# A fixed place in a 20-place period for each background piece of the first attention of a gated two-layer kernel

## What is computed

```python
x = x + jnp.tanh(g_xattn[0]) * _L0_xattn_ref(_layernorm(x, axis=-1), ctx_1024, ...)
x = x + jnp.tanh(g_ffn[0]) * _L0_ffn_ref(_layernorm(x, axis=-1), ...)
x = x + jnp.tanh(g_xattn[1]) * _L1_xattn_ref(_layernorm(x, axis=-1), ctx_1024, ctx_1024)
x = x + jnp.tanh(g_ffn[1]) * _L1_ffn_ref(_layernorm(x, axis=-1), ...)
```

```python
q = query @ Wq.T + bq          # k, v from key_value in the same way
scores = jnp.einsum('bhqd,bhkd->bhqk', q, k) / np.sqrt(HD).astype(np.float32)
s = jnp.where(x >= 0, x + 1.0, 1.0 / (1.0 - x))
attn = s / jnp.sum(s, axis=-1, keepdims=True)
context = jnp.einsum('bhqk,bhkd->bhqd', attn, v)
return context @ Wo.T + bo
```

## Time and profile before

| | us |
|---|---|
| median of 3 runs | 1206.94 (1204.21 to 1207.81) |
| the profiled execution, device time | 1198.75 |
| its span, first to last instruction | 1196.9 |
| PE, DVE, ACT, POOL busy | 1012.3, 791.6, 624.9, 382.4 |
| first attention (28.4 to 339.8 us of the span) | 311.4 |
| its tail to the barrier (339.8 to 398.4 us) | 58.6 |

### The profile page before, as it was taken

One profiled execution on the slowest core, in us unless ns is written; L12 is line 12 of the kernel. 1 busy time (PEld: TensorE's weight loads), 2 busy tenths in 40 slices (PEclk: granted clock), 3 DMA queues, 4 the chain that ended last, 5 costly groups with the idle time before them and its releaser, 6 DMA issues.

```text
span 1196.9 us, 16849 instructions
## 1 busy us (share of the span) xinstructions
PE 1012.3 (85%) x5379; PEld 713.5 (60%) x5379; DVE 791.6 (66%) x2003; ACT 624.9 (52%) x1205; POOL 382.4 (32%) x385
## 2 busy tenths in 40 slices
PE   4898798698875679989899976888898988898988
PEld 2454454354444567878687754546575766666666
DVE  5777877866777757664657566776667577664443
ACT  2776656757846425564654431364555455544542
POOL 6000000000000013777767722224344343524134
PEclk9898979979997889999999995989999999999999
DMA  6654542632121433888877653331312232120001
GB/s 155 172 149 125 163 137 62 178 117 53 50 106 53 145 108 94 185 216 223 215 192 178 140 135 78 102 100 27 107 49 81 56 91 80 53 58 1 21 1 36
DMA packets 101559, 128.38 MB, mean 107 GB/s; under 512 B 31136, under 2 KB 73504, under 8 KB 101216
## 3 DMA queue, kind: packets, MB, share of 16 engines
q1 hardware_dynamic: 87088, 106.32, 31.1%
q0 software_dynamic: 12288, 18.88, 8.8%
q10 hardware_dynamic: 2096, 2.10, 0.8%
HBM read 66.15 MB, written 30.70 MB: 81 GB/s over the span
## 4 chain that ended last, share of the span: by engine, by line
PE 52%; DVE 27%; ACT 7%; issue 6%; POOL 3%; DMA 2%; ACTq 1%; SPq 1%; DVEq 0%; POOLq 0%
PE psum L951 5%; PE psum L1135 5%; PE psum L1120 5%; PE psum L1040 4%; PE psum L858 4%; PE psum L967 4%; PE psum L829 3%; DVE stats L1405 3%; DVE peaks L1815 3%; DVE weights L1530 3%; PE psum L904 3%; PE psum L818 2%; PE psum L1067 2%; PE psum L853 2%; PE psum L775 2%
## 5 line engine op out<-in xcount | busy, mean ns | idle before, releaser
L1914 POOL TENSOR_SCALAR vareps<-moments 128x4 f32<-128x4 f32 x32 | 10.4, 326 | 477.5 <-DVE moments L1414 477.5
L829 PE MATMUL psum<-q_stack,k_stack 97*128 97x512 f32 (+1 forms) x256 | 119.0, 493 | 38.6 <-DVE weights L1530 21.4
L1341 ACT ACTIVATE weights<-psum 128x512 f32<-128x512 f32 x160 | 92.9, 595 | 65.8 <-PE psum L829 57.5
L1934 POOL DMA_INDIRECT expert_sums<-made,sum_rows x64 | 103.3, 1614 | 61.1 <-DVE made L1779 42.6
L1067 PE MATMUL psum<-k_stack,q_stack 96*128 96x308 f32 x256 | 86.1, 397 | 36.4 <-DVE peaks L1815 24.2
L1530 DVE SCALAR_TENSOR_TENSOR weights<-weights,psum 128x512 f32<-128x512 f32 x160 | 101.8, 679 | 21.4 <-ACT weights L1196 21.3
L1815 DVE TENSOR_REDUCE peaks<-psum 128x2 f32<-128x308 f32 x256 | 105.6, 469 | 9.3 <-PE psum L1067 9.2
L1191 ACT ACTIVATE weights<-psum 128x512 f32<-128x512 f32 x160 | 88.8, 595 | 29.2 <-PE psum L829 28.9
L951 PE MATMUL psum<-feat_parts,w_shared_up 128*128 128x512 f32 x384 | 98.3, 406 | 6.4 <-DVE shared_silu L1653 2.8
L1966 POOL TENSOR_TENSOR hidden<-hidden_whole,hidden 128x512 fp32r<-128x512 f32 x64 | 82.9, 1300 | 61.0 <-DVE hidden L1863 61.0
L1135 PE MATMUL psum<-w_con_high,hidden 128*128 128x256 f32 x512 | 101.2, 296 | 0.5 <-POOL hidden L1966 0.5
(11 more groups left out here) (211 smaller groups left out, 2204.7 us busy)
## 6 DMA issues: line engine op xcount, KB each, us to landing
expert_w<-in_expert_w SPq DMA_DIRECT2D x64, 384.0 KB
q_stack<-q_stage SPq DMA_DIRECT2D x96, 128.0 KB, 2.4
q_stack<-q_stage SPq DMA_DIRECT2D x174, 64.0 KB, 2.0
expert_sums<-zeros SPq DMA_DIRECT2D x6, 1408.0 KB, 8.3
fetched<-expert_sums SPq DMA_DIRECT2D x14, 512.0 KB, 4.6
k_raw<-in_k SPq DMA_DIRECT2D x16, 300.0 KB
x<-in_x SPq DMA_DIRECT2D x8, 512.0 KB, 4.7
rows_scratch<-rows SPq DMA_DIRECT2D x8, 512.0 KB, 2.9
```

The lines of the kernel that those rows point to most:

```text
L829: T.matmul(to, keys_of(h, head), q[0:row, head // 2, :], start=True, stop=True).then_inc(scored, 1)
L1341: A.activation(weights1[n % 6][:, :], score_bank[n % 2], ACT.Exp).then_inc(exped, 1)
L1934: G.indirect_dma_start(sum_dram[e % SUMS], bass.IndirectOffsetOnAxis(ap=sum_rows[:, e:e + 1], axis=0), made[e % 4][:, :], None, bounds_che ...
```

## The change

The three streams are gone from the attention loop. Each step of the background has a number, its place relative to the half, in four tables, and a step that falls behind the last place goes to the tail. The steps are also cut finer: `stats` is split into the measuring (`bn`, two tiles each) and the rest, `norm` into two, `q_parts` into `q_high` and `q_low`, `shift` into `highest` and `shift`, and `position` gives its last four operations to `ranks`. No instruction is added or taken out; they stand elsewhere.

```diff
+SLOTS = 5 * GROUPS
+LAST_SLOT = SLOTS * HALVES + 6
@@
+Q_AT = (-34, -26, -24, -21, -21, -20, -19, -19, -17, -17, -17, -16, -16)
+K_AT = (-16, -15, -8, -7, -6, -5)
@@
+    for h in range(HALVES):
+        first = SLOTS * h
+        put(att_steps(h), first, A_AT)
+        put(route_steps(h), first, R_AT)
+        if h + 1 < HALVES:
+            put(query_steps(h + 1), first + SLOTS, Q_AT)
+        if h % 2 == 0 and h + 2 < HALVES:
+            put(keys_steps(h // 2 + 1), first + 2 * SLOTS, K_AT)
@@
     def step():
-        for stream in (early, keyed, late):
-            stream.step()
+        plan.extend(slots.pop(next(now_at), []))
@@
-        late.step()
+        late.step(len(late.steps) // (TAIL_TILES - i) + (len(late.steps) % (TAIL_TILES - i) > 0))
```

More of the change, by code:

```diff
@@ L173, in query_steps @@
 def query_steps(h):
-    return [[("stats", "q", h), ("rstd", "q", h)], [], [("norm", "q", h)], [("turn_q", h)],
-            [("q_feats", h)], [("project_q", h, 0)], [("q_parts", h, 0), ("project_q", h, 1)], [("q_parts", h, 1)],
-            [("send_q", h)]]
-def after_steps(h):
-    turn, divide = [("normalize", h, t) for t in range(HT)], [("divide", h, t) for t in range(HT)]
-    b, last = h // TOGETHER_GATED, h % TOGETHER_GATED == TOGETHER_GATED - 1
-    return [turn[0:2], divide[0:2] + turn[2:4], divide[2:4], [("turn_att", h)], [("att_feats", h)],
-            [("project_o", h, 0), ("project_o", h, 1)], [("x_add", h, 0), ("x_add", h, 1)],
-            [("stats", "r", h), ("rstd", "r", h)], [], [("norm", "r", h)], [("turn_rows", h), ("send_rows", h)],
-            [("row_feats", h)], [("gate", h)], [("shift", h)], [("top", h)], [("pick", h)],
-            [("gate_exp", b)] if last else [], [("count", h)], [("position", h)], [("gate_weights", b)] if last else []]
+    return norm_steps("q", h) + [[("turn_q", h)], [("q_feats", h)], [("project_q", h, 0)], [("q_high", h, 0)],
+                                 [("q_low", h, 0)], [("project_q", h, 1)], [("q_high", h, 1)],
+                                 [("q_low", h, 1), ("send_q", h)]]
@@ new lines, in att_steps, with route_steps @@
+def att_steps(h):
+    steps = []
+    for t in range(HT):
+        steps += [[("normalize", h, t)], [("divide", h, t)]]
+    return steps + [[("turn_att", h)], [("att_feats", h)], [("project_o", h, 0)], [("x_add", h, 0)],
+                    [("project_o", h, 1)], [("x_add", h, 1)]]
+def route_steps(h):
+    b, last = h // TOGETHER_GATED, h % TOGETHER_GATED == TOGETHER_GATED - 1
+    return norm_steps("r", h) + [[("turn_rows", h), ("send_rows", h)], [("row_feats", h)], [("gate", h)],
+                                 [("highest", h)], [("shift", h)], [("top", h)], [("pick", h)],
+                                 [("count", h), ("gate_exp", b)] if last else [("count", h)], [("position", h)],
+                                 [("ranks", h), ("gate_weights", b)] if last else [("ranks", h)]]
@@ L194, in plan_first @@
     queries.step()
+    queries.step()
+    queries.step()
     plan += [("load_x", 1), ("load_rest",)]
@@ L234, in plan_first @@
             plan.append((("weigh", q, 0), ("weigh", q, 1), ("keep", q))[i % 3])
-            if i % 3 == 2 and q % GROUPS == GROUPS - 1:
-                late.add("after", after_steps(q // GROUPS))
         after = sets[i + 2] if i + 2 < len(sets) else []
```

77 lines of the change are left out of this document (44 added, 33 removed).

## The result

The changed kernel takes 1162.83 us (median of four runs, 1160.95 to 1164.33), the kernel before beside it 1205.58 (1203.89 to 1207.81): a ratio of 0.9655 with a 95% interval of 0.9624 to 0.9687, or 42.8 us less. The prediction had the sign, and less than half the size: 17 us, with a range that ended at 1171.

What follows compares the result with a forecast made beforehand. Three engines of nearly equal load spend 10 us of a half waiting for each other. Middle halves -21.6, half 1 +1.6, half 0 -2.2, half 6 +1.6, tail +3.5 make -17.1: median 1189.8 us, range 1171 to 1206.

Steps and rivals of the forecast that it cites:

- Fourth group: Last group of a middle half: q_parts, pick, count and one project_q leave, so 13.5 becomes 9.5 us.
- The second group: Second group of a middle half: two x_add waits go and DVE's backlog is worked off, 9.4 becomes 8.0 us.
- The first: First group of a middle half: DVE becomes the bound with 12.5 us of work, 9.6 becomes 12.8.
- The third: Third group of a middle half: ACT's own five chunks set it, 10.9 becomes 7.0 us.
- it keeps the fall of the clock: At the second project_q of a middle half, PE idles up to about 3 us; 1.2 added per half at 1.2 GHz.
- rival A: Middle halves: the clock falls in the light groups too, half 41.8 us, total about 1209, no change; chance 0.14.
- The keys: Sending keys six places before their half: nothing, or up to 3 us in three halves.
- Half 0 and the start: Half 0 loses later queries and keys (-4.3), but its first queries leave 2.1 later; net -2.2 us.
- Half 6: Half 6 takes over the last pieces of query work, 32.4 to 34, +1.6 us.
- The tail: Behind the last weight: half 6's gate operations 2.7 and a POOL wait 1.8, less 1.0 for mixing, +3.5 us.
- C: Halves reach what their busiest engine needs, 34.5 us; four save 37.6, total 1170; chance 0.13.
- B: First group: PE stops at the second project_q for the bank behind the count; +18, 1225 us; chance 0.09.

Runs made afterwards that it cites:

- the doubled transposes: Kernel before with the 16 transposes of each normalize done twice, nothing else changed; ratio 0.9985 (0.9966 to 1.0004) against the kernel before.
- the coarse kernel: Changed kernel at its new places, with query measuring, normalize pairs, both project_o, and ranks with position joined again; ratio 0.9973 against the kernel before.
- the single joinings: Changed kernel with only ranks, second normalize, second project_o or query measuring joined again, one per run; ratios 0.9746, 0.9758, 0.9743, 0.9693 against the kernel before.

## Why the prediction was right in sign and short in size

**The loss it saw was there.** The prediction read the middle halves as three nearly equal engines waiting for each other, and put the gain there. It was there, and the four waits it named (before `q_feats`, the scores, the divides and `x_add`) are the ones that went or shrank. Busy time over the four halves hardly moved for DVE and ACT, at about 129 and 110; idleness went. The sizes of the terms follow.

**Fourth group: 9.5 forecast, 6.0 measured. This is the step that failed most, 3.5 in each of four halves.** It set what remains in the group at 7 for ACT, the 9.61 less two table loads, and took one `project_q`, 2, off the 10.9 of PE. Both left work in that goes. Rows of before in the fourth group of half 4 (218.5 to 232.0), line, engine, operation and count, then busy time and mean ns:

```profile
L818 PE MATMUL psum<-q_feats,wq 128*128 128x512 f32 x8 | 3.9, 605 | 0.0
L800 PE MATMUL psum<-wv,ctx_t 128*128 128x256 f32 x8 | 1.9, 379 | 0.0
...
L1220 ACT ACTIVATE probs<-probs 128x1024 f32<-128x1024 f32 x1 | 1.1, 1057 | 1.6 <-DVE masks L1583 1.6
```

Both `project_q` (L818) stood there, 3.9 together, and both have left it, as the first-group part of the prediction itself has it. The `values` of the keys (L800), 1.9, and the count have left too, and the 2.0 of the gate's logits have come in. In after PE is busy 5.01 in the group, where the forecast left it 8.9. On ACT `gate_exp` (1.1, 0.3 and 0.2) goes with the two table loads; without all of it 5.5 of the 9.61 remain, and after shows 5.55. So the load of the group was mis-sized, on PE by 3.9. A smaller part is where the window is cut: the scores of one fifth chunk, 0.9, fall just outside of this one in after. Windows cut by DVE's weights put such pieces of PE on one side or the other, so the sum over a half is the safer one.

The second group, 8.0 forecast and 7.0 measured, failed in the same way. The forecast took waits of DVE off it, but PE was its full engine (9.07 of 9.40) and is so now (7.00 of 7.00), with most of `turn_att` and, in half 4, the key matmuls (0.48) gone from it. The first (12.8 forecast, 12.4 measured) held, with DVE at 11.85 for the 12.5 summed. The third (7.0 and 6.8) held in number only: ACT was to set it, and DVE fills it, with 6.80 of 6.80 beside ACT's 6.20.

**The clock: "it keeps the fall of the clock" was wrong.** The step took up to 3 of PE idleness at the second `project_q`, and 1.2 per half for the fall behind it. The timeline of half 4's first group in after (L836 is `project_q`, L893 `normalize`, L906 `turn_att`):

```profile
169.98 0.75 DVE L1555 SCALAR_TENSOR_TENSOR q_stage<-psum,bq,q_stage 128x512 fp32r<-128x512 f32 x1
...
170.79 1.99 PE L836 MATMUL psum<-q_feats,wq 128*128 128x512 f32 x4 [0.50 <-DVE q_stage L1555]
172.21 0.80 PE L847 MATMUL psum<-q_stack,k_stack 97*128 97x512 f32 x1
...
173.10 0.60 ACT L1209 ACTIVATE weights<-psum 128x512 f32<-128x512 f32 x1 [1.20 <-PE psum L847]
...
174.83 2.12 PE L893 MATMUL psum<-ident,turned 128*128 128x128 f32 x12
...
178.21 0.60 ACT L1178 ACTIVATE row_feats<-psum 128x512 f32<-128x512 f32 x1 [2.50 <-PE psum L906]
```

PE waits 0.50 there, and 0.86 at the same place of half 2. The forecast summed DVE's list up to `q_low` as if PE stood idle beside it from the start, while PE had the first `project_q` (1.98), a weigh part (1.02), the scores and the count to do in the same time. The clock rows of after show no stretch at 1.2 GHz between 61.7 and 304.0, so the change also got what the doubled transposes price at about 10, where the forecast kept a loss of 1.2 a half.

The Trainium skill, page "TensorE: Matmul & The Clock Gate", section "A second HAM failure mode: psum-queue depth-cycling", which the prediction set beside rival A, says that a PE which idles briefly but often between groups of matmuls, while it cycles through PSUM banks, has its clock swing between the two levels. This trace does not show that at its amount of idleness: PE still idles 12.0 of 140.0 us in the middle halves, in single waits of up to 1.06, and the clock stays at 1.00. Before, it idled 25.1 of 175.7, at 0.87. So rival A did not occur.

**The keys** were named ("in every other half the keys") and given no price. They add 3.1 to the first group and 2.3 to the third of an odd half (15.5 and 9.1, beside 12.4 and 6.8 in an even one). The forecast gave all four halves one length. The mean of 35.0 hides 32 and 38.

**Half 0 and the start.** The first queries leave 4.2 later than before (24.76 for 20.55) where 2.1 was forecast. The two key masks stand on DVE between `q_high` (15.32) and `q_low` (19.23) of the first pair, as the forecast had it; it did not count that the second `project_q` and its pair then come behind both. The first weight is late by 3.5 (33.2 for 29.7):

```profile
19.23 0.74 DVE L1555 SCALAR_TENSOR_TENSOR q_stage<-psum,bq,q_stage 128x512 fp32r<-128x512 f32 x1
...
20.02 3.13 PE L836 MATMUL psum<-q_feats,wq 128*128 128x512 f32 x4 [2.69 <-DVE q_stage L1555]
...
24.76 5.90 SPq L750 DMA_DIRECT2D q_stack<-q_stage  x9
```

PE's second `project_q` waits 2.69 for the first pair's parts, which come behind the masks. But half 0, counted from its own first weight, is 10 shorter (26.5 for 36.4), where the forecast took 4.3 off it, so in sum the first half ends 6.5 earlier, not 2.2. By groups, 7.1 of that 10 lie in the third and fourth (5.7 and 5.7 for 8.4 and 10.1). With the queries at their old places these two are 7.8 and 9.5, with the keys at theirs 7.0 and 6.7, with the output and the gate at theirs 5.7 and 5.7; so it is mostly the queries.

**Half 1** took 36.6 where 37 was forecast. **Half 6** was forecast to grow by 1.6, and stayed (32.1 for 32.4). **Half 7** was forecast unchanged and is 2.4 shorter (27.8 for 30.2); the gate of half 6 has left it for the tail.

**The tail** grew by 3.9 where 3.5 was forecast, and by the operations that were named: the gate of half 6 starts behind the last weight, and the first norm waits for POOL within its step. The DVE rows of it (L1591 is `highest`, L1582 `x_add`, L1478 the norm):

```profile
296.07 0.42 DVE L1591 TENSOR_REDUCE top_logit<-psum 128x4 f32<-128x256 f32 x1
...
313.84 0.75 DVE L1582 SCALAR_TENSOR_TENSOR x<-psum,tanh_gates,x 128x512 f32<-128x512 f32 x1 [3.68 <-PE psum L922]
...
316.63 0.75 DVE L1582 SCALAR_TENSOR_TENSOR x<-psum,tanh_gates,x 128x512 f32<-128x512 f32 x1 [1.11 <-PE psum L922]
...
322.48 0.73 DVE L1478 TENSOR_SCALAR rows<-x,moments,rstd 128x256 f32<-128x256 f32 x2 [1.63 <-POOL rstd L1956]
```

The wait for POOL is 1.63 for the 1.8 forecast. Half 7's gain and the tail's loss look like one move seen twice, of which the forecast counted the second alone.

**The sum, to the first barrier:** halves 0 and 1, -6.5 + 1.3; halves 2 to 5, -35.7; halves 6 and 7, -0.3 and -2.4; tail +3.9; together -39.7 beside -39.9 read off. The forecast for the same was -17.1. Of the 22.6 between, 14.1 lie in the middle halves; there the four groups and the clock together were forecast 6.3 too long in each half (3.5 of it the fourth group, 1.0 the second, 1.2 the clock), and the keys, not counted, took 11 of these 25 back. The rest is half 0 (4.3), half 6 (1.9), half 7 (2.4) and half 1 (0.3), less 0.4 of the tail.

**The rivals.** C, the halves reaching what their busiest engine needs, is what happened in the middle halves, at 1170 forecast and a chance of 0.13. Its half was written as 34 + 1 = 34.5; with the 35 that the terms make, four halves save 35.6, and 35.7 came. Its total still fell short, by what halves 0, 6 and 7 gave. What spoke against it in the text, 12.5 of DVE in one group, was no argument: the half's total counts. B, PE stopping at the bank behind the count, is real as a mechanism. It does not occur at the places chosen, and does with places one step off, though at the second `normalize` and not at the second `project_q`: there the coarse kernel shows 2.16 and 5.10. At the second `project_q` itself it occurs in half 5 with `q_high` on ACT, with a wait of 2.54 and a first group of 20.2 for 15.5. With all four joinings the loss is 37 us, and the kernel ends just level with before, not above it. (B's half of 43.9 + 0.3 is 0.5 over its own terms, 37.3 + 3 + 3.4; it changes nothing.)

**What isn't settled.** The cut alone is worth 9 to 12 in the middle halves, the new places with coarse pieces also 9, both together 35.7. That the two need each other is shown; why the single joinings add up so evenly (35.5 for 37.3) although they sit in different groups isn't. Nor was the one-place shift of each family tried in the other direction, nor work taken off PE, which would show whether PE or DVE is the floor now.

## What to carry to other kernels

Where engines with nearly equal loads work through one list in order and share a small ring of banks, sum each engine's load over a whole period to find the floor, and take that floor as a real candidate for the forecast. Then look for each piece that waits for a bank and ask what stands behind it on its engine; here one such piece one place early cost up to 11 us over eight halves. Cutting pieces and moving them were worth little apart here (9 to 12 and 9 of 35.7); that only small pieces fit between a wait and what stands behind it is the likely reason, not a shown one.

## What the runs showed of the hardware

More work on TensorE made a stretch shorter: 64 additional transposes in the kernel before raised the mean granted clock of four halves from 0.87 to 0.98, and they took 165.6 for 175.7.

Pauses of like length were followed by a fall of the clock in one place and not in another. It fell behind 1.26 and 1.49 in before, both within four chunks. It did not fall in the middle halves of after, where single waits of PE reach 1.06, and only once in those with the second `normalize` early, where they reach 1.17. And what a fall costs is not fixed: 14.5 fewer us at 1.2 GHz in the middle halves of the coarse kernel gave 0.9 there.

In the second group of after PEld is busy 4.42 of 7.00 while the matmuls fill 7.00. The Trainium skill, page "Perfetto Trace Analysis", section "Identifying the Most-Contended Engine", calls the busy share of the matmul row no good measure of how near TensorE is to its limit, as matmuls are pipelined, and would go by its share of peak FLOPs and by the weight loads. By the loads it has a third to spare here. No run here took matmul work away, and with `q_high` on ACT DVE's work in this group stayed the same (5.49 for 5.51), so which row is the truer one stays open.
